# Graph network on one core: the norm behind the relational layers moved into the third layer, the last norm into the output stage, and two banks in the projections and heads

## What is computed

```
x = _layernorm(x + _L0_gnn_ref(x, ...))   # four graph convolutions
x = _layernorm(x + _L1_gnn_ref(x, ...))   # attention of 4 heads, a state space scan, gates
x = _layernorm(x + _L2_gnn_ref(x, ...))   # three relational layers
x = _layernorm(x + _L3_gnn_ref(x, ...))   # attention of 2 heads, a linear layer
```

## Time and profile before

| | us |
|---|---|
| median of 3 runs | 7617.66 |
| fastest and slowest of them | 7611.27, 7618.0 |
| the profiled execution, its own time | 7593.99 |
| span from its first to its last instruction | 7592.3 |

### The profile page before, as it was taken

How to read it: one execution, slowest core, us unless ns; L and a number is a source line. 1 busy time by engine, 2 the same in 40 slices (tenths; PEclk the granted TensorE clock), 3 DMA queues, 4 the chain that set the end, 5 groups by cost and what they waited for, 6 DMA issues and landing times. The chain is left out here.

```text
span 7592.3 us, 88522 instructions
## 1 busy us (share of the span) xinstructions
PE 4466.2 (59%) x19132; PEld 2331.9 (31%) x19133; DVE 3997.3 (53%) x6221; ACT 1808.3 (24%) x2757; POOL 2364.8 (31%) x2280
## 2 busy tenths in 40 slices
PE   4887575209992463759556776566774444430583
PEld 2453474103441222635223333223332122220121
DVE  8976474999995894245222332222331111228995
ACT  1574011107872322334001111001110000010352
POOL 0000000400000452000566665666665666630000
PEclk8998687659995776979667887678886666665897
DMA  1471674426662674145555556555665444453443
GB/s 41 160 241 41 222 250 141 154 66 202 180 169 96 222 262 171 59 144 207 163 165 171 187 190 183 157 166 180 195 194 146 135 137 139 138 135 119 139 135 107
DMA packets 505240, 1197.38 MB, mean 158 GB/s; under 512 B 66602, under 2 KB 289653, under 8 KB 492498
## 3 DMA queue, kind: packets, MB, share of 16 engines
q1 hardware_dynamic: 330558, 586.57, 23.9%
q0 software_dynamic: 141200, 464.73, 20.8%
q10 hardware_dynamic: 33396, 145.09, 5.3%
HBM read 924.69 MB, written 274.66 MB: 158 GB/s over the span
## 5 line engine op out<-in xcount | busy, mean ns | idle before, releaser
L2607 POOL DMA_INDIRECT rel1s_rows<-rel_table,rel1s_at x672 | 650.6, 968 | 402.1 <-issue 340.1
L2607 POOL DMA_INDIRECT rel0s_rows<-rel_table,rel0s_at x672 | 652.2, 971 | 380.9 <-issue 346.0
L2607 POOL DMA_INDIRECT rel2s_rows<-rel_table,rel2s_at x672 | 645.5, 961 | 368.9 <-issue 328.9
L2739 PE MATMUL rel2s_acc<-rel2s_rows,rel2s_hot 128*128 x764 | 410.7, 550 | 470.2 <-issue 413.6
L2126 POOL TENSOR_TENSOR mamb_st<-mam_u,mamb_bc 128x1600 f32<-128x1600 f32 x64 | 228.3, 3567 | 1143.3 <-DMA mamb_bc<-dbc 1143.3
L1677 PE MATMUL gatx_acc<-gatx_w,gatx_feat 128*65 128x400 f32 x1600 | 541.0, 501 | 25.1 <-DVE gatx_w L1569 25.1
L2739 PE MATMUL rel0s_acc<-rel0s_rows,rel0s_hot 128*128 x764 | 348.6, 472 | 306.7 <-issue 252.7
L2739 PE MATMUL rel1s_acc<-rel1s_rows,rel1s_hot 128*128 x764 | 341.8, 464 | 293.1 <-issue 230.2
L1569 DVE SCALAR_TENSOR_TENSOR gatx_w<-gatx_w,gatx_adj 128x1600 f32<-128x1600 f32 x200 | 363.3, 1817 | 0.5 <-ACT gatx_w L1625 0.5
L1416 DVE CUSTOM_DVE_ANT_0 gatm_junk<-gatm_srow,gatm_gone 128x3200 bf16<-128x3200 f32 x100 | 343.5, 3489 | 33.5 <-DMA gatm_srow<-gat_scores 29.1
L1677 PE MATMUL latx_acc<-latx_w,latx_feat 128*65 128x400 f32 x800 | 291.9, 509 | 100.6 <-DVE latx_w L1569 100.6
(11 more groups left out here) (611 smaller groups left out, 9572.2 us busy)
## 6 DMA issues: line engine op xcount, KB each, us to landing
mamb_bc<-dbc SPq DMA_DIRECT2D x128, 800.0 KB, 5.8
agg_strip<-strips SPq DMA_DIRECT2D x100, 800.0 KB, 5.8
gatx_adj<-adj SPq DMA_DIRECT2D x200, 400.0 KB, 3.1
adj<-adj_counts SPq DMA_DIRECT2D x25, 1600.0 KB, 7.1
latx_adj<-adj SPq DMA_DIRECT2D x100, 400.0 KB, 3.1
rel_table<-rel0p_prod POOLq DMA_DIRECT2D x25, 1536.0 KB, 6.2
rel_table<-rel0s_prod ACTq DMA_DIRECT2D x25, 1536.0 KB
rel_table<-rel1s_prod ACTq DMA_DIRECT2D x25, 1536.0 KB
```

The lines of the kernel that those rows point to most:

```text
L2607: pool.indirect_dma_start(rows[:, u, k, :], None, table, bass.IndirectOffsetOnAxis(ap=at[:, n:n + 1], axis=0)).then_inc(s_in[u], 16)
L2739: one = nc.tensor.matmul(acc[a][:, :], to, row[:, 0:2 * D], start=fresh and k == 0, stop=False)
```

## The change

The change makes three edits.

1. Two banks. `project` has two product banks in turn instead of one, so a product waits for the eviction of tile t-2; `heads_to_nodes` lets the transposes of tile t begin when tile t-2 is evicted, with two divisor tiles.
2. The third relational layer (`gather_sum` with `last`) loads all of x at its start, adds x to the sigmoid of each tile, takes the statistics inside DVE's step of a tile two later (`summed`), and normalises 23 tiles while the last tile's edges are gathered and the last two behind them (`factors` on DVE, `scaled` on ACT). SP stores x in two DMAs. The stage reln is gone, as is `rel_h`. The weights of the last block are loaded and transposed at the start of the third layer.
3. The last output stage loads all of x at its start and does product, bias, relu, addition and norm in four groups, as gcno does, and stores the output from there. The stage lasn and `last_h` are gone.

```
 def project(...):
-        mm = [ph.ps(f"mm{n}", [P, BANK]) for n in range(NC)]
+        mm = [[ph.ps(f"mm{u}_{n}", [P, BANK]) for n in range(NC)] for u in range(2)]
...
-            pe.sem_inc(s_done, NC)
+            pe.sem_inc(s_done, 2 * NC)
...
-                pool.wait_ge(s_done, (t + 2) * NC)
+                pool.wait_ge(s_done, (t + 3) * NC)
...
 def heads_to_nodes(...):
-        den = ph.sb("den", [P, H])
+        dens = [ph.sb(f"den{u}", [P, H]) for u in range(2)]
...
             pe.sem_inc(s_t, 2)
+            pe.sem_inc(s_o, 1)
...
-def gather_sum(nc, name, g, table, own, out=None, then=None):
+def gather_sum(nc, name, g, table, own, then=None, last=None):
...
-            s_act = ph.sem("act")
+            x_dram, x_out, beside = last
+            x = ph.sb("x", [P, T, D])
...
+            parts = [(0, T - 2), (T - 2, T)]
+            beside.banks(ph, name)
...
         def _(sp):
             if then:
                 for to, a in load_weights(w):
                     sp.dma_start(to, a).then_inc(s_w, 16)
+            else:
+                sp.dma_start(x[:, :, :], nodes(x_dram)).then_inc(s_x, 16)
+                beside.load(sp)
...
+            if not then:
+                beside.loaded(sp)
+                for k, (a, b) in enumerate(parts):
+                    sp.wait_ge(s_out, b)
+                    sp.dma_start(nodes(x_out)[:, a:b, :], x[:, a:b, :]).then_inc(s_st[0], 16)
+                sp.wait_ge(s_st[0], 32)
...
             def evict(t, u, i):
...
-                    dve.wait_ge(s_st[u], (i + 1) * 16)
+                    dve.wait_ge(s_add, t + 1)
...
+            def summed(t, u):
+                dve.wait_ge(s_act, t + 1)
+                mine = x[:, bass.ds(t, 1), :].rearrange("p a d -> p (a d)")
+                nc.vector.tensor_tensor(res[u][:, :], res[u][:, :], mine, ALU.add).then_inc(s_both, 1)
+                dve.wait_ge(s_both, t + 1)
+                dve.sem_inc(g.waited, 1)
+                nc.vector.tensor_copy(mine, res[u][:, :])
+                nc.vector.bn_stats(stats[u][:, :], res[u][:, :]).then_inc(s_bn, 1)
+                dve.wait_ge(s_bn, t + 1)
+                dve.sem_inc(g.waited, 1)
+                nc.vector.bn_aggr(pairs[u][:, :], stats[u][:, :]).then_inc(s_add, 1)
+                dve.wait_ge(s_add, t + 3)
+                dve.sem_inc(g.waited, 1)
+                nc.vector.tensor_copy(mv[:, bass.ds(t, 1), :].rearrange("p a k -> p (a k)"), pairs[u][:, :]).then_inc(s_var, 1)
+
+            def factors(k):
+                a, b = parts[k]
+                dve.wait_ge(s_std, k + 1)
+                nc.vector.reciprocal(std[:, a:b], std[:, a:b]).then_inc(s_v, 1)
+                dve.wait_ge(s_v, k + 2)
+                nc.vector.scalar_tensor_tensor(less[:, a:b], mv[:, a:b, 0], -1.0, std[:, a:b], ALU.mult, ALU.mult).then_inc(s_rec, 1)
+
+            if not then:
+                nc.vector.memset(eps[:, :], EPS).then_inc(s_v, 1)
+                dve.sem_inc(s_add, 2)
+                dve.wait_ge(s_x, 16)
 
             def step(t, u, i, second):
...
                 edges(t, first, 2)
                 evict(t - 1, 1 - u, i)
+                if not then and second:
+                    summed(t - 2, u)
+                    if isinstance(t, int):
+                        factors(0)
...
+            else:
+                summed(T - 2, 1)
             evict(T - 1, 0, T // 2)
+            if not then:
+                summed(T - 1, 0)
+                factors(1)
...
         def _(pe):
...
+            else:
+                beside.turn(pe)
...
         def _(act):
...
+                beside.copy(act)
+                act.wait_ge(s_v, 1)
...
             def store(t, u):
...
                     nc.scalar.activation(res[u][:, :], res[u][:, :], ACT.Sigmoid).then_inc(s_act, 1)
-                    act.wait_ge(s_act, t + 1)
-                    act.sem_inc(g.waited, 1)
-                    act.dma_start(out[bass.ds(a, P), :], res[u][:, :]).then_inc(s_st[u], 16)
+
+            def scaled(k):
+                a, b = parts[k]
+                act.wait_ge(s_var, b)
+                nc.scalar.activation(std[:, a:b], mv[:, a:b, 1], ACT.Sqrt, bias=eps[:, 0:1]).then_inc(s_std, 1)
+                act.wait_ge(s_rec, k + 1)
+                for t in range(a, b):
+                    nc.scalar.activation(x[:, t, :], x[:, t, :], ACT.Identity, bias=less[:, t:t + 1], scale=std[:, t:t + 1]).then_inc(s_out, 1)
...
+            else:
+                scaled(0)
             store(T - 1, 0)
...
+            else:
+                scaled(1)
...
 def last_attention(...):
...
+                sp.dma_start(x[:, :, :], nodes(x_dram)).then_inc(s_x, 16)
+                for k, (a, b) in enumerate(GROUPS):
+                    sp.wait_ge(s_o, k + 1)
+                    sp.dma_start(nodes(out[0:whole * P, :])[:, a:min(b, whole), :], x[:, a:min(b, whole), :]).then_inc(s_st, 16)
...
+                dve.wait_ge(s_x, 16)
+
+                def before(_, a, b):
+                    mine = [k for k, pr in enumerate(pairs) if a <= pr[0] < b]
+                    for k in mine:
...
+                    dve.wait_ge(s_r, mine[-1] + 1)
+                    v(nc.vector.scalar_tensor_tensor(x[:, a:b, :], o[:, a:b, :], 0.0, x[:, a:b, :], ALU.max, ALU.add))
+                norm.dve(nc, dve, v, x, before=before, done=s_o)
-    residual_norm(nc, "lasn", x_dram, h_dram, out)
```

More of the change, by code:

```diff
@@ L783, in multiply @@
                     for k in range(2):
-                        last = nc.tensor.matmul(mm[n][:, 0:b - a], turned[u][:, k, :], weights[:, k, a:b],
+                        last = nc.tensor.matmul(mm[u][n][:, 0:b - a], turned[u][:, k, :], weights[:, k, a:b],
                                                 start=k == 0, stop=k == 1)
@@ L2518, in _, with relational_stack @@
                 beside.copy(act)
-def relational_stack(nc, g, before, x_dram, weights, roots, biases, h):
+def relational_stack(nc, g, before, beside, x_dram, weights, roots, biases, x_out):
     L = 3
@@ L2543, in relational_stack @@
             else:
-                gather_sum(nc, f"rel{n}s", g, tables[n % 2], own, out=h)
-def gather_sum(nc, name, g, table, own, out=None, then=None):
+                gather_sum(nc, f"rel{n}s", g, tables[n % 2], own, last=(x_dram, x_out, beside))
+def gather_sum(nc, name, g, table, own, then=None, last=None):
     B, R = G_SUM, SLOTS
@@ L2578, in gather_sum @@
         else:
-            s_act = ph.sem("act")
+            x_dram, x_out, beside = last
+            x = ph.sb("x", [P, T, D])
+            stats = [ph.sb(f"stats{u}", [P, 6]) for u in range(2)]
+            pairs = [ph.sb(f"pairs{u}", [P, 2]) for u in range(2)]
+            mv = ph.sb("mv", [P, T, 2])
+            std, less, eps = (ph.sb(n, [P, T]) for n in ("std", "less", "eps"))
+            s_x, s_act, s_both, s_add, s_bn, s_var, s_std, s_rec, s_out, s_v = ph.sems(
+                "x", "act", "both", "add", "bn", "var", "std", "rec", "out", "v")
+            parts = [(0, T - 2), (T - 2, T)]
+            beside.banks(ph, name)
         block = ph.block()
@@ L2644, in evict @@
                 if isinstance(t, int) and t == 0:
-                    if not then:
-                        dve.wait_ge(s_st[u], 16)
                     dve.sem_inc(s_part, 1)
@@ L2846, in _ @@
         def _(act):
-            for u in range(2):
-                act.sem_inc(s_st[u], 16)
+            if then:
+                for u in range(2):
+                    act.sem_inc(s_st[u], 16)
+            else:
+                beside.copy(act)
+                act.wait_ge(s_v, 1)
             def top(t, u, i):
@@ L2896, in _, with last_attention @@
                 middle(T - 1, 0)
+            else:
+                scaled(0)
             store(T - 1, 0)
-            act.wait_ge(s_st[0], (T - T // 2 + 1) * 16)
-            act.wait_ge(s_st[1], (T // 2 + 1) * 16)
-def last_attention(nc, g, before, x_dram, W, a_l, a_r, bias, lin_w, lin_b, out):
+            if then:
+                act.wait_ge(s_st[0], (T - T // 2 + 1) * 16)
+                act.wait_ge(s_st[1], (T // 2 + 1) * 16)
+            else:
+                scaled(1)
+def last_attention(nc, g, weights, WT, x_dram, a_l, a_r, bias, lin_w, lin_b, out):
     H = 2
@@ L2960, in _, with before @@
             def _(act):
-                for k, pr in enumerate(pairs):
-                    act.wait_ge(s_t, k + 1)
-                    nc.scalar.copy(turned[k % 2][:, 0:len(pr) * P], tp[k % 2][:, 0:len(pr) * P]).then_inc(s_c, 1)
+                def before(group):
+                    low = GROUPS[group + 1][0] if 0 < group < len(GROUPS) - 1 else 0 if group == 0 else T
+                    high = GROUPS[min(group + 1, len(GROUPS) - 1)][1]
+                    for k, pr in enumerate(pairs):
+                        if low <= pr[0] < high:
+                            act.wait_ge(s_t, k + 1)
+                            nc.scalar.copy(turned[k % 2][:, 0:len(pr) * P], tp[k % 2][:, 0:len(pr) * P]).then_inc(s_c, 1)
```

(1 more changed line is left out.)

52 lines of the change are left out of this document (26 added, 26 removed).

## The result

The changed kernel took 7535.81 us (median of 4 runs, 7534.68 to 7544.03) where the kernel before took 7617.83 in the same comparison (4 runs, 7611.27 to 7618.37): a ratio of 0.9897, with a 95% interval of 0.9879 to 0.9914. That is 82 us between the medians, and 78 (66 to 92) by the ratio; 73 were forecast. The two profiled executions are only 50 us apart (7592.3 and 7542.4).

What follows compares the result with a forecast made beforehand. It took no engine to bound the whole kernel, a row of stages with a barrier behind each. 42.9 - 11.0 - 3 - 2 + 35 + 11.1 = 73.0 us off the median 7617.66 gave 7545, range 7512 to 7588.

Steps and rivals of the forecast that it cites:

- The stage removed: Norm behind the relational layers moved inside the third layer: its 46.9 us go, about 4.0 return; gain 42.9, between 40 and 44.
- The load of x ahead of the first row numbers: Third layer's start: DVE waits for all of x before writing the first row numbers; cost 11.0, between 10 and 13.
- The loop: Third layer's loop: about 1.7 us more DVE work per tile, mostly covered by the gathers; cost 3, between 0 and 31.
- The last tile: Third layer's end: 3 MB are stored while the last chunk's rows are landing; cost 2, between 0 and 6.
- The last norm: Last norm moved into the output stage, last activation 41.8 us behind the first eviction; gain 35, between 32 and 38.
- a wait for x in this stage: Output stage: x was to land no later than the first product; a wait for it would show the forecast wrong.
- The banks: Two banks in the five small stages (projection and heads), until store or load loops bind; gain 11.1, between 2 and 25.
- (a): Small stages: stores and loads already set the period, so the banks give nothing; 7556 us, chance 0.20.
- (c): Small stages: the banks give all that the evictions cost, 90 us instead of 11; 7466 us, chance 0.05.
- (b): Third layer's loop: the added DVE work is not hidden, 41 us where 3 were taken; 7583 us, chance 0.12.
- (d): Third layer: DVE's longer step adds one 8.0 us stop per tile ahead of the row numbers; 7735 us, chance 0.03.
- (e): Third layer's start: the x load holds nothing up, landing while the layer starts; 7534 us, chance 0.05.

Runs made afterwards that it cites:

- the first comparison: Each of the three edits alone, and all together, against the kernel before (7590.87 us): banks 0.9981, norm in the layer 0.9966, norm in the output stage 0.9954, all 0.9901.
- the added copies: The changed kernel with 15 or 40 unread, chained DVE copies more per tile of the third layer: 7590.31 us (0.9953) and 7835.68 us (1.0286).
- third comparison: Against the kernel before (7588.97 us), the changed kernel with four buffers and one bank 0.9902, both layer-start holders moved 0.9885, SP's increment alone 0.9894, all that helped 0.9780.
- the second: Against the kernel before (7620.50 us), the changed kernel with x's wait moved 0.9895, 15 extra copies 0.9953, 40 copies 1.0286, four buffers 0.9810.

## Why the prediction was right

Its sum was 73.0. It came near both by its mechanisms, which the runs bear out for all three edits, and by some luck: 5 us set aside for the loop and the last tile were not needed, and what the output stage, the tail and the load of x missed makes 3.6 the other way. Term by term:

- **The stage removed: 42.9, measured 42.0.** The change of table and the activations lie as forecast. What was missed is SP's queue. SP waits in its own loop for the landings of all gathers and comes to the 23-tile store only at 6749.48, 15 us after its tiles were ready; the two-tile store then stands behind it. That makes the tail 8.2 us where 3.3 + 4.0 was the estimate.
- **The load of x ahead of the first row numbers: 11.0, measured 12.4 as a wait**, and 11.3 in the distance between the gathers of the two layers (a mean of 46.9 in three profiles with the edit, 35.7 in three without). The size is right and the cause was half of it: the load was the later of two holders, and taking it away alone shows the other.
- **The loop: 3 between 0 and 31, measured 0** within a few us, in the first comparison (979.9 and 984.3 with the additions, 983.5 and 983.7 without). The argument, that row numbers are needed four gathers later, understated the cover, which is some 8 to 11 us per tile beyond the change.
- **The last tile: 2, for 3 MB of store beside the last gathers; it did not happen.** The store was issued 5.9 us after the last gather's start (6743.6), since SP came late. Two misses, this and the 0.9 above, have one cause, and offset each other in part.
- **The last norm: 35 between 32 and 38, measured 32.6** in the trace and 35 (25 to 46) in the run of its own. x came 0.9 us late, from 13.1 to landing where gcno showed 11.05, and the small loads ahead of the heads' sum took 0.9 longer than before. The prediction had named a wait for x in this stage as a sign that the forecast is wrong, and by that sign this term failed: DVE stands 4.20 us for x, of which 0.9 delays the first eviction. The rest, 42.8 from first eviction to last activation against 41.8, is a small error. TensorE was at 0.50 until some 7498, at 1.00 from 7502 to 7506, and at 0.50 again at 7514. gcno, at 0.50 throughout, gave 33.1 as the other bound; it was the better estimate. In the kernel with four buffers, where TensorE was granted 0.86 to 1.00 from 7430 to 7442, the same stage took 61.6 us where this one took 65.1.
- **The banks: 11.1, measured 12.5** in the traces and 14 (8 to 21) in the run. The terms were mis-sized both ways: locp 3.6 where 1.8 came, loch 3.2 where 5.3 came, gcnp 3.5 and 3.7, lasp 0.3 and 0.7, lash 0.5 and 1.0. That they add up to nearly the right sum is luck. For locp I had taken the landing at 2.1 us; in the trace with two banks its median is 2.2 and its longest 3.0.

By the traces that makes 42.0 - 11.3 + 32.6 + 12.5 = 75.8, and the runs gave 75 and 78. The prediction was made against the median and not against the profiled execution, 23.7 lower. That was right for the comparison it was made for: its like would have been 7521, which those runs never reached. In the first comparison, where the kernel before had 7590.87, the changed one had 7515.25.

One of its sums was wrong. With each bound on its own side the gain is 44 - 10 - 0 - 0 + 38 + 25 = 97 at most and 40 - 13 - 31 - 6 + 32 + 2 = 24 at least, so the times reach from 7521 to 7594 and not from 7512 to 7580, and the stated range (up to 7588) doesn't take in all of its own bounds. The result lies inside either.

Of the rivals, (a) and (c) fell with the banks alone (14, between 8 and 21), and the buffers show why neither holds. The Trainium skill (Perfetto Trace Analysis, Matmuls) says that independent matmul groups should rotate through PSUM banks. The changed kernel's trace agrees in loch, where PE's waits for the eviction are gone, and not in locp, where they rose from 2.0 to 8.0 us; and in both, loads and stores kept most of the time. With four buffers, 81.7 of the 90 that rival (c) had worked out came. (b) and (d) fell with the added copies, (e) with the timelines.

## What to carry to other kernels

A pipelined loop has as many loops in it as it has kinds of buffer, and its period is that of the longest. Work out all of them from the rows and widen those that are close together at once: here each alone gave 9 to 12.5 us, and both 82. When an engine's first instruction is late, list everything that its release depends on, the increments that stand in another engine's program behind slow issues too; a wait that the profile names is only the last of them. And price a gain that one profile shows against code that the edit does not touch, since here 12 us came and went in a layer whose code was the same in both.

## What the runs showed of the hardware

- A small load issued on SP directly behind the load of all of x (3.3 MB in 25 tiles) held SP's sequencer for 5.1 to 5.7 us, in gcno (5.19 before, 5.41 after) and in the third layer (5.26 to 5.74 in eleven profiles). The load of x itself held it for 0.37 to 0.40 there, and the same weights behind smaller loads took 0.56. What is programmed behind waits.
- The same 3.3 MB landed in 11.7 to 12.1 us at the third layer and in 13.1 to 13.8 in the output stage, where gcno's had taken 11.05.
- The second relational layer's gathers spanned 1010 to 1014 us in the first and third comparison and 1020 to 1027 in the second, with the same code, and the kernel before took 7590.87 and 7588.97 us against 7620.50. The first and third ran on one chip, the second on another. Whether the chip is the cause was not tried.
- DVE stopped for up to 2.5 us, mostly 1 to 2.5, between two equal copies in a row with no releaser that the profile shows, 49 times with 375 copies and 66 times with 1000. What it waits for there stays open.
